# A two-phase transformer kernel: second MLP product of the first phase in three bf16 terms, and a new order of work on all engines

## The reference

```python
q_prob, k_prob = _prob(q), _prob(k)          # tanh * 0.499 + 0.5, divided by the row sum
log_ratio = jnp.log(q_prob) - jnp.log(k_prob)
sid = jnp.einsum('bnd,bmd->bnm', q_prob - k_prob, log_ratio)
attn = jax.nn.softmax(-sid / D ** 0.5, axis=-1)
f_diff = (v - jnp.einsum('bnm,bmd->bnd', attn, v)) @ W_diff.T + b_diff + q
h = _layernorm(f_diff, ln_g, ln_b)
mlp = jax.nn.gelu(h @ W1.T + b1, approximate=False) @ W2.T + b2
out = _layernorm(mlp + f_diff, ln_g, ln_b)
```

## Time and profile before

| what | value |
|---|---|
| time, median of 3 runs | 1747.3 us (1745.95 to 1748.33) |
| the profiled execution's own time | 1748.64 us |
| its span, first to last instruction | 1746.9 us |
| PE busy | 1607.0 us (92%) |
| DVE busy | 1368.7 us (78%) |
| ACT busy | 1056.6 us (60%) |
| POOL busy | 942.5 us (54%) |
| first phase | from 0 to about 670 us of the span |
| first 5 us, ACT | 4 table loads |
| second phase | from about 676 us to the end |

### The profile page before, as it was taken

One profiled execution on the slowest core, in us unless ns is written; L12 is line 12 of the kernel. 1 busy time (PEld: TensorE's weight loads), 2 busy tenths in 40 slices (PEclk: granted clock), 3 DMA queues, 4 the chain that ended last, 5 costly groups with the idle time before them and its releaser, 6 DMA issues.

```text
span 1746.9 us, 42800 instructions
## 1 busy us (share of the span) xinstructions
PE 1607.0 (92%) x14411; PEld 1258.5 (72%) x14411; DVE 1368.7 (78%) x3213; ACT 1056.6 (60%) x1894; POOL 942.5 (54%) x1329
## 2 busy tenths in 40 slices
PE   5999999999999992677999999999999999999997
PEld 4888888888888882444777777767777777767666
DVE  5688888888888866768888888888888888887642
ACT  6666666666666553255656666665666666565654
POOL 5555666566655635224556465555646465564535
PEclk9999999999999996688999999999999999999999
DMA  6322212221122002342323232332223232333200
GB/s 211 101 62 74 76 60 60 74 76 60 60 73 77 7 1 71 96 123 78 83 81 91 78 96 74 90 86 83 80 84 91 74 94 79 86 85 86 62 15 20
DMA packets 215099, 133.59 MB, mean 76 GB/s; under 512 B 45937, under 2 KB 214257, under 8 KB 214769
## 3 DMA queue, kind: packets, MB, share of 16 engines
q1 hardware_dynamic: 215024, 132.61, 26.1%
HBM read 101.07 MB, written 25.17 MB: 72 GB/s over the span
## 4 chain that ended last, share of the span: by engine, by line
PE 42%; ACT 8%; issue 6%; DVE 3%; SPq 1%; POOL 1%; DMA 0%; ACTq 0%; POOLq 0%
PE b_bank L1637 23%; PE b_bank L1716 7%; PE b_scoreT L1694 4%; PE b_score L1677 3%; PE b_scoreT L1698 3%; ACT L31 3%; ACT b_E L1275 2%; ACT b_Y L1335 2%; PE b_bank L1645 1%; ACT b_xT L1281 1%; PE b_bank L1731 1%; DVE b_nm L1457 1%; SPq L1086 0%; SPq L1097 0%; PE b_scoreT L1662 0%
## 5 line engine op out<-in xcount | busy, mean ns | idle before, releaser
L1457 DVE TENSOR_REDUCE b_nm<-b_score 128x4 bf16<-128x1024 f32 x256 | 314.5, 1228 | 121.1 <-PE b_score L1677 115.2
L1275 ACT ACTIVATE b_E<-b_scoreT 128x1024 f32<-128x1024 f32 x256 | 262.2, 1024 | 191.1 <-PE b_scoreT L1698 190.3
L1199 POOL TENSOR_SCALAR b_YT<-b_Y 128x512 bf16<-128x512 f32 x128 | 85.9, 671 | 292.0 <-ACT b_Y L1335 282.5
L760 PE MATMUL bank<-W2T,G 128*128 128x256 f32 x1024 | 231.2, 379 | 0.0
L760 PEld LDWEIGHTS bank<-W2T,G 128*128 128x128 f32 x1024 | 192.1, 190 | 24.8
L31 ACT ACT_TABLE_LOAD x156 | 200.1, 1283 | 9.8 <-PEq L875 6.4
L1335 ACT ACTIVATE b_Y<-b_bank,b1f 128x256 f32<-128x256 f32 x256 | 107.5, 471 | 160.0 <-PE b_bank L1637 159.6
L1637 PE MATMUL b_bank<-b_hT,f 128*128 128x256 bf16 x1536 | 189.9, 274 | 11.4 <-ACT b_Y L1335 11.4
L1637 PE MATMUL b_bank<-f,b_YT 128*128 128x256 bf16 x1536 | 184.0, 273 | 2.5 <-POOL b_YT L1202 1.6
L727 PE MATMUL bank<-hT,W1T 128*128 128x256 bf16 x1536 | 178.3, 273 | 6.4 <-ACT G L497 2.5
L1637 PEld LDWEIGHTS b_bank<-b_hT,f 128*128 128x128 bf16 x1536 | 143.3, 98 | 54.7 <-ACT b_Y L1335 19.7
(11 more groups left out here) (209 smaller groups left out, 3455.6 us busy)
## 6 DMA issues: line engine op xcount, KB each, us to landing
b_Q<-q_dram SPq DMA_DIRECT2D x256, 64.0 KB, 2.5
b_K<-k_dram SPq DMA_DIRECT2D x256, 64.0 KB, 2.5
xin<-in_x SPq DMA_DIRECT2D x32, 256.0 KB, 4.5
ctxn<-in_ctx SPq DMA_DIRECT2D x32, 256.0 KB, 2.8
mask_in<-in_mask SPq DMA_DIRECT2D x32, 256.0 KB, 3.0
X<-in_x SPq DMA_DIRECT2D x32, 256.0 KB, 4.4
ctxt<-in_ctxT SPq DMA_DIRECT2D x32, 256.0 KB, 4.6
b_ctxt<-in_ctxT SPq DMA_DIRECT2D x32, 256.0 KB, 2.8
```

The lines of the kernel that those rows point to most:

```text
L760: last = nc.tensor.matmul(out_ps[:, t], G[w.parity][:, h, t * P:(t + 1) * P], W2T[:, h], start=h == 0, stop=h == HC - 1)
L1275: nc.scalar.activation(E[:, pair:pair + 2], scoreT_ps[:, :, :, :], ACT.Exp).then_inc(sig["E"], 1)
L1457: nc.vector.tensor_reduce(pair, score_ps[:, :, :, :], AX.X, ALU.max, negate=True).then_inc(sig["nm"], 1)
```

## The change

In the first phase the second MLP product is done as the first one was: `W2T` and the GELU values are split into bf16 high and rest (`GT`), and `output` becomes a `product` over three terms. The high parts of the values are made by ScalarE (`gelu_high`, four copies of 128x512 in an iteration), the rests by subtraction, one of four by VectorE and three by GpSimd (`gelu_low`). The float32 weights are loaded into the buffer that later holds `G`, and split once, in iteration 4, by a copy on ScalarE and a subtraction on VectorE. `G` has one buffer in place of two. `output(0)` waits for all four rests before it starts; before, it waited for the GELU values pair by pair.

The negated means are dropped: GpSimd subtracts the mean instead. Two small copies on VectorE (`rs1`, `mu1`) are now reductions over an axis of length one. All pieces are named functions, and each engine calls them in a new order.

```diff
-        W2T = sb("W2T", [P, HC, D], F32, late)
+        W2T = sb("W2T", [P, 2, HC, D], BF16, late)
...
-        G = two("G", [P, HC, S], F32)
+        G = sb("G", [P, HC, S], F32)
+        GT = sb("GT", [P, 2, HC, S], BF16)
+        raw_2 = G[:, :, :].rearrange("p h s -> p (h s)").rearrange("p (h d) -> p h d", h=HC)
...
-                    last = nc.gpsimd.tensor_scalar(dst[:, t, :], src[:, t, :], neg[:, t:t + 1], rs[:, t:t + 1],
-                                                   ALU.add, ALU.mult)
+                    last = nc.gpsimd.tensor_scalar(dst[:, t, :], src[:, t, :], mv[:, t, 0:1], rs[:, t:t + 1],
+                                                   ALU.subtract, ALU.mult)
...
+                def gelu_high(j):
+                    act.wait_ge(sig["G"], done(m, per=HC // 2, part=j + 1))
+                    if j == 0:
+                        if (due := done(m, back=1)) is not None:
+                            act.wait_ge(sig["out_mm"], due)
+                    nc.scalar.activation(GT[:, 0, 2 * j:2 * j + 2], G[:, 2 * j:2 * j + 2], ACT.Copy).then_inc(sig["Ghi"], 1)
...
+                if at_batch(q, 2):
+                    act.wait_ge(sig["W2_in"], 16)
+                    nc.scalar.activation(W2T[:, 0], raw_2, ACT.Copy).then_inc(sig["W2hi"], 1)
+                if at_batch(n, 4):
+                    load_functions(nc, act, GELU_AND_TANH)
+                    act.wait_ge(sig["rows_in"], 16 * 5)
+                    nc.scalar.activation(gate[:, :], gate_raw[:, :], ACT.Tanh).then_inc(sig["gate"], 1)
+                if q:
+                    context_product()
+                load_functions(nc, act, LN_AND_EXP)
...
+                def gelu_low(j):
+
+                    dve.wait_ge(sig["Ghi"], done(m, per=HC // 2, part=j + 1))
+                    nc.vector.tensor_tensor(GT[:, 1, 2 * j:2 * j + 2], G[:, 2 * j:2 * j + 2], GT[:, 0, 2 * j:2 * j + 2],
+                                            ALU.subtract).then_inc(sig[f"Glo{j}"], 1)
...
                 def output(t):
-                    for h in range(HC):
-                        if t == 0 and h % 2 == 0:
-                            pe.wait_ge(sig["G"], done(w, per=HC // 2, part=h // 2 + 1))
-                        last = nc.tensor.matmul(out_ps[:, t], G[w.parity][:, h, t * P:(t + 1) * P], W2T[:, h],
-                                                start=h == 0, stop=h == HC - 1)
-                    return last
...
+                        for j in range(HC // 2):
+                            pe.wait_ge(sig[f"Glo{j}"], done(w))
+                    last = product(out_ps[:, t], lambda s, k: GT[:, s, k, t * P:(t + 1) * P], lambda s, k: W2T[:, s, k],
+                                   range(HC))
...
+                if at_batch(m, 0):
+                    pe.wait_ge(sig["W1"], 1)
```

More of the change, by code:

```diff
@@ L489, in iteration, with gelu, store_x @@
                     last.then_inc(sig["th"], 1)
[L490 to L500, removed]
+                def gelu(j):
+                    act.wait_ge(sig["mlp_mm"], done(m, per=HC // 2, part=j + 1))
+                    if j == 0 and at_batch(m, 0):
+                        act.wait_ge(sig["W2"], 1)
+                    if (due := done(m, back=1)) is not None:
+                        act.wait_ge(sig[f"Glo{j}"], due)
+                    for i in range(2):
+                        last = nc.scalar.activation(G[:, 2 * j + i], mlp_ps[j % 2][:, i], ACT.Gelu,
+                                                    bias=b1c[:, 2 * j + i:2 * j + i + 1])
+                    last.then_inc(sig["G"], 1)
+                def gelu_high(j):
+                    act.wait_ge(sig["G"], done(m, per=HC // 2, part=j + 1))
+                    if j == 0:
+                        if (due := done(m, back=1)) is not None:
+                            act.wait_ge(sig["out_mm"], due)
+                    nc.scalar.activation(GT[:, 0, 2 * j:2 * j + 2], G[:, 2 * j:2 * j + 2], ACT.Copy).then_inc(sig["Ghi"], 1)
+                def store_x():
                     act.wait_ge(sig["x1"], done(w))
@@ L777, in iteration, with scores @@
                     transposed(lT_ps, lr[u.parity], "lT_mm")
[L778 to L787 removed]
+                def scores():
                     pe.wait_ge(sig["dT"], done(u))
@@ L845, in iteration @@
                     last.then_inc(sig["att_mm"], 1)
-                if m:
+                if at_batch(m, 0):
+                    pe.wait_ge(sig["W1"], 1)
+                if at_iteration(half, parity, NB + 2):
+                    pe.wait_ge(sig["base"], NB)
+                    pe.wait_ge(sig["peak_w"], 1)
+                    nc.tensor.transpose(U_ps[0:1, 0, 0:P], peak_w[:, :], ident[:, :]).then_inc(sig["peak_rows"], 1)
+                if u:
+                    logs_transposed()
+                    difference_transposed()
+                if q:
+                    context_product()
+                if w:
+                    output(0)
+                if u:
+                    scores()
+                if m:
+                    mlp_transposed()
+                if w:
+                    output(1)
+                if m:
+                    hidden(0)
+                if u:
+                    exponentials_transposed()
+                if m:
+                    hidden(1)
                     hidden(2)
                     hidden(3)
+                if u:
+                    attention()
+                if at_iteration(half, parity, NB + 2):
+                    pe.wait_ge(sig["peak_all"], 1)
+                    nc.tensor.matmul(U_ps[:, 1, 0:1], second["ones"][:, :], peak_all[:, :], start=True, stop=True).then_inc(
+                        sig["peaks_w"], 1)
                 if at_batch(q, 1):
```

269 lines of the change are left out of this document (167 added, 102 removed).

## The result

The changed kernel took 1823.09 us (median of 4 runs, 1820.62 to 1824.01), the kernel before 1746.68 us beside it (4 runs, 1745.95 to 1748.33). The ratio is 1.0434, 95% interval 1.0416 to 1.0452. I had forecast 1726 us, so the sign is wrong. The profiled execution took 1822.18 us with a span of 1820.4, which is 73.5 us more than the span before.

What follows compares the result with a forecast made beforehand. PE was taken as the bound in the first phase. 26 iterations x 1.29 = 33.5 us, less 14.4 for filling, plus 2 for emptying, gave 21 us gained: 1726 us, likeliest range 1714 to 1737, about 0.8 held from 1712 to 1741.

Steps and rivals of the forecast that it cites:

- The product: Second MLP product on PE: two float32 halves of 3.46 us become 48 bf16 instructions, 2 x 2.62 = 5.24 us.
- the wait ahead of the scores: PE stands 0.76 us every middle iteration: ACT's chain from U to the scores 5.11 us, PE's cover 4.35.
- the floor: PE's own work in a middle iteration falls to 17.41 us; the order decides what is added.
- The rival of the whole gain: Table load or copies fit PE's cover, so the 0.76 us wait does not appear: 20 us less, 1706 us; chance 0.07.
- the filling: Early iterations: iteration 5 some 14.5 us late (bounds 9 and 19), iteration 8 some 14.4 us late.
- the wait for the bias product: Iteration 7: PE waits for the bias product's correction on DVE, some 1.7 us more than before.
- The emptying: From iteration 34 on: about 2 us of waiting for the last rests against faster products; a gain of 2 us taken.
- the likeliest case: Whole kernel: chance 0.70, own range 1714 to 1737 us, from filling 5 either way, lock and chain allowances.
- The lock: DVE operations stretched beside POOL subtractions: priced at nothing in the likeliest case, 0.4 us an iteration at its upper end.
- the 18.6 to 18.9 us of the rival: The lock becomes the iteration's limit: 18.6 to 18.9 us, 11 to 19 us more, 1737 to 1745 us; chance 0.15.
- the chain: Middle iteration: from PE's start on U through ACT's copies and table load to the scores, 5.11 us; iteration 18.17.
- a slower kernel: Rival that the changed kernel is slower than before; chance 0.06.

Runs made afterwards that it cites:

- the swapped order: Changed kernel with the attention sum and its statistics ahead of the output norm's update on VectorE: 1800.41 us, ratio 1.0302.
- the kernel with two buffers: Changed kernel with two buffers each for `stx` and `mvx`, and `row_maximum` at the end of VectorE's iteration: 1832.27 us, ratio 1.0477.
- the kernel with the table load first: Changed kernel with negated means back and ScalarE's logarithm and exponential table load ahead of the copy of U: 1707.4 us, ratio 0.978.

## Why the prediction was wrong

**The step that failed** is one clause: "The renamed subtractions of the mean and the reductions of length one change no duration that PE sees". The reductions indeed cost nothing. For the subtraction I had a row of the add form (0.56 us) and none of the subtract form, and put no bound on it. It takes 1.22 us. With the negated means back, and nothing else, the kernel is at 1728.7 us. The two kernels are 94 us apart, and that is all but 3 us of the error: 1823.1 - 1726 = 97.

**From 2.65 us to 3.4 an iteration.** The closed path can be followed in the rows. From the start of `vef` to the end of `rso` POOL takes 324.44 + 0.81 - 309.65 = 15.60 us. From there DVE takes over: the update of x, its statistics, the attention sum and `mvf`. The next `vef` starts at 331.42, 6.17 us later. Together that is 21.77 us, and the middle iteration is 21.78. POOL's three rests run beside DVE's part and are not on the path. With negated means POOL's part is 308.03 + 0.71 - 296.39 = 12.35 us and DVE's about 4.5. The path is then some 16.9 us long (an estimate from these rows), under the 18.20 that PE and ACT set, so it doesn't bind.

The path grew by 4.9 us, and the first 1.3 were free. POOL's part grew by 3.25: the four normalisations 2.26 (5.06 in place of 2.80), `df` 0.45, `veo` 0.45 and `rso` 0.10. DVE's grew by 1.7, the two updates of x (2.61 in place of 0.88). All but the 2.26 falls beside work of the other engine, but no run takes one such collision away alone. That they come from the other engine's work is read from what overlaps.

Two other kernels agree with this path. Two fast instructions in it give 1.35 us back, and a rest of 0.61 us in DVE's part adds 0.60, though it took work off POOL. That the wait for `mvf` binds is shown by the swapped order, too; that the waits for `stx` and the row maximum don't, by the kernel with two buffers.

**What was right.** The product (2.62 us a half), the wait ahead of the scores and, within 0.3 us, the floor. In the changed kernel itself the product and the wait stand in iterations 5 and 6, before the work on `xh1`, which begins at 94.9 us, tells on PE. Timeline of PE:

```profile
66.00 0.60 PE L876 MATMUL bank<-ident,lr 128*128 128x128 f32 x4
...
71.86 1.99 PE L870 MATMUL bank<-lT,dT 128*128 128x256 f32 x8 [0.46 <-ACT dT L472]
...
84.15 0.60 PE L876 MATMUL bank<-ident,lr 128*128 128x128 f32 x4
...
102.29 0.60 PE L876 MATMUL bank<-ident,lr 128*128 128x128 f32 x4
110.78 2.08 PE L945 MATMUL bank<-raw,bv_rep 128*128 128x256 f32 x4 [7.45 <-DVE bv_rep L822]
113.37 3.78 PE L870 MATMUL bank<-WdT,ctxt 128*128 128x256 f32 x8 [0.52 <-DVE gbo_all L686]
...
132.53 0.60 PE L876 MATMUL bank<-ident,lr 128*128 128x128 f32 x4
```

84.15 - 66.00 = 18.15 us, forecast 18.17. The rival of the whole gain, put at 1706 us, lies beside the 1707.4 of the kernel with the table load first, but by luck: the middle gave 12 us of the 20 that the rival had, and the filling, where it had nothing, 12 more.

**Terms of the wrong size.** Iteration 5 began at 66.00, 11.5 us late in place of 14.5. Iteration 7 took more than that back: I had 1.7 us for the wait for the bias product and 0.8 for ACT, but PE waited 7.45 us, because its operand `bv_rep` stands behind the probabilities on DVE. Behind that wait the bias product and U ran at a granted clock of 0.50, and U took 3.58 us from start to start in place of 1.73. The two errors cancel in the kernel with negated means, where iteration 8 starts at 129.86 and the sum of my steps gives 115.0 + 14.4 = 129.4. The emptying was to give 2 us and gave none: from iteration 34 to the product of the maxima it takes 655.01 - 603.14 = 51.9 us there, 51.4 before. So the first phase gives 672.31 - 655.01 = 17.3 us there, of 21 forecast; that its 1728.7 us lie so near 1726 is in part the second phase, which I had put at nothing. Two readings of mine were off besides. The range of the likeliest case doesn't follow from its terms, which give 1716 to 1741 and not 1714 to 1737. And that the first U runs at the low clock rested on its 3.75 us alone: the profile gives a granted clock of 1.00 from 12.9 to 16.7 us. For the next two the doubt was right: in the changed kernel U takes 3.62 us from 21.33 on, at a granted clock of 0.50, and 3.10 from 47.06 on, at 0.61.

**The lock.** In the likeliest case I priced it at nothing. With the fast form that held, at 15.2 us of POOL in 18.20 and even at 15.8 in 17.69. The 0.4 us an iteration at the upper end and the 18.6 to 18.9 us of the rival were estimates of mine that no run shows: with negated means the iteration is 18.20 us where the chain gives 18.17, and the chances of 0.15 for that rival and 0.06 for a slower kernel were judged, not worked out from a row. What the runs show in their place depends on what lies beside what. In the changed kernel the four operations on `pr`, from 310.02 us on, take 1.38 us, 0.41 each, though two powers begin at 309.95 and 310.93, while the updates of x take 1.34 in place of 0.48 beside the rests. PE waits 2.00 us for the rests ahead of `output(0)`, which I had named as a sign that I am wrong. But the rests take 1.27 us each, 0.11 more than the 1.16 of the earlier trace rows; they are late because they start late, behind the subtractions. What I left out was that this lengthening switches on: once POOL is late, long operations of both engines fall on each other in every iteration, x on the rests, and DVE's rest (1.30 us, 0.69 with negated means) on POOL's sums and `veo` (0.67 in place of 0.22).

## What to carry to other kernels

A "renamed" operation is a new instruction: if the trace doesn't show its exact form on its engine, its cost has no row, and the range must reach to the nearest slow one. Multiply a doubt on one instruction by its count in an iteration, and compare it with the slack of the closed path that it lies on, not with the engine's free time. Here 4 x 0.66 = 2.6 us stood against 3 us of room on POOL at 83% and would have passed. The path through both engines, from `mvf` over `rso` back to `mvf`, had only 1.3. In the kernel before, the same slow instructions left the iteration at 19.46 us. Where an operation grows beside one of another engine, as the update of x did (1.34 us in place of 0.48), ask which operations start together if one of the two engines is late by a microsecond, not only what they take on average.

## What the runs showed of the hardware

- GpSimd's `tensor_scalar` on 128x256 float32 with per-partition operands: add and multiply 0.55 us, subtract and multiply 1.22, multiply and subtract 1.22, subtract alone 0.92. Whether the operand lies densely or two columns apart made no difference (0.553 and 0.548 us).
- Its `tensor_tensor` doesn't show such a penalty as far as rows go: the subtraction of two 128x512 tiles takes 1.16 us, and the sum of two of 128x256 0.72.
- An update of 128x256 on VectorE beside GpSimd's subtractions of 128x512 took 1.34 us in place of 0.48. One began 0.12 us into a subtraction of 1.15 and ended 0.29 us after it.
- Beside a power on two columns this wasn't seen. VectorE's `nrden` (two columns) took 1.19 us in the kernel before (median of 32; one stood beside a subtraction in the earlier trace rows), and 0.17 us in the kernel with negated means, where it began at 308.11, inside a power from 308.03 to 308.74.
- In the kernel with the attention sum first, TensorE waits 2.1 to 2.4 us ahead of the scores in every iteration. In two of three the scores then take 1.83 us (granted clock 1.00 from 307.74 to 309.57), and behind the third 3.41 (0.53 from 327.77 to 331.18). In the changed kernel the iteration from 324.27 to 346.11 us had a mean granted clock of 0.92 and the one from 280.72 to 302.56 had 1.00, and both lasted 21.84 us: the lower clock cost nothing where TensorE would have waited anyway.
